# Seven quarter products for eight in three of eight blocks of a quantized FFN's second product, the residual added by GpSimd, and some waits rearranged

## What is computed

```python
fused = concat([x, mean(x, axis=1), cond, cond], -1)         # 4 x 1024 x 1536
r = relu(fused @ cond_W + cond_b)                            # 512 wide
h = relu(quant_linear(r, w1, b1))                            # FFN1: 512 -> 2048
y = quant_linear(h, w2, b2)                                  # FFN2: 2048 -> 512
out = x + y
def quant_linear(x, w, b):
    s_in = max(x) / 255;  xq = clip(round(x / s_in), 0, 255) * s_in
    s_w  = rowmax(|w|) / 127;  wq = clip(round(w / s_w), -128, 127) * s_w
    return xq @ wq.T + round(b / (s_in * s_w)) * (s_in * s_w)
```

## Time and profile before

| what | us |
|---|---|
| median of 3 executions (326.12 to 329.09) | 326.31 |
| the profiled execution, its own device time | 326.76 |
| its span in the profile | 325.0 |
| PE busy (share of the span) | 315.9 (97%) |
| DVE busy | 256.5 (79%) |
| ACT busy | 205.3 (63%) |
| POOL busy | 95.2 (29%) |

### The profile page before, as it was taken

The page is one execution under the profiler, slowest core; times in us unless marked ns, Lnnn a source line. Parts: engine busy times, 40 slices in busy tenths (PEclk is TensorE's granted clock), DMA queues, the critical chain, the costliest instruction groups (busy, mean ns, idle before and its releaser), DMA issues.

```text
span 325.0 us, 4331 instructions
## 1 busy us (share of the span) xinstructions
PE 315.9 (97%) x1491; PEld 180.3 (55%) x1491; DVE 256.5 (79%) x541; ACT 205.3 (63%) x364; POOL 95.2 (29%) x80
## 2 busy tenths in 40 slices
PE   6999999999998999999999999899999999999995
PEld 6888888888685444444444444344444444444444
DVE  1698988997888999999999999844569665665665
ACT  2445695578376993466666663199996959568300
POOL 1076524644223999970370002600000000000000
PEclk9999999999999999999999999999999999999999
DMA  7999999999963397995990150379969799567042
GB/s 224 207 248 245 231 194 242 258 244 321 310 126 68 66 275 35 356 417 243 416 419 7 70 192 0 131 304 422 408 233 415 287 357 382 175 221 289 0 161 99
DMA packets 51622, 75.54 MB, mean 232 GB/s; under 512 B 20344, under 2 KB 34960, under 8 KB 46864
## 3 DMA queue, kind: packets, MB, share of 16 engines
q1 hardware_dynamic: 51408, 74.99, 76.7%
q10 hardware_dynamic: 192, 0.28, 0.4%
HBM read 45.89 MB, written 25.17 MB: 219 GB/s over the span
## 4 chain that ended last, share of the span: by engine, by line
PE 79%; DVE 11%; DMA 4%; issue 2%; ACT 1%; SPq 1%; DVEq 0%
PE bank L734 34%; PE bank L632 20%; PE bank L507 17%; PE bank L604 6%; DMA pool_q<-in_L_ffn_w_dram 2%; DVE wmax L927 2%; DVE hidden L1049 2%; DMA x_in<-in_x_dram 1%; SPq L304 1%; DVE hidden L910 1%; PE bank L502 1%; DVE hidden L915 1%; DVE pool_r L1024 1%; DVE w_sum L992 1%; ACT pool_r L790 1%
## 5 line engine op out<-in xcount | busy, mean ns | idle before, releaser
L734 PE MATMUL bank<-w_t,pool_q 128*128 128x512 f16 x256 | 55.9, 379 | 0.2 <-DVE pool_q L1144 0.2
L734 PE MATMUL bank<-w_t 128*128 128x512 f16 (+1 forms) x272 | 55.9, 366 | 0.0
L1159 DVE TENSOR_TENSOR bank<-bank,ends_b 128x512 f32<-128x512 f32 (+1 forms) x33 | 22.5, 681 | 38.8 <-PE bank L734 38.7
L1049 DVE TENSOR_SCALAR_CACHE_REDUCE hidden<-bank,qb,hmax 128x512 f32<-128x512 f32 x62 | 47.6, 809 | 4.4 <-PE bank L632 3.8
L424 POOL TENSOR_TENSOR x_lo<-hidden,x_hi 128x512 fp32r<-128x512 f32 x28 | 35.4, 1300 | 45.5 <-ACT x_hi L771 45.5
L507 PE MATMUL bank<-x_lo,cw_hi 128*128 128x512 f32 x128 | 48.4, 389 | 0.0
L507 PE MATMUL bank<-x_hi,cw_lo 128*128 128x512 f32 x128 | 48.4, 389 | 0.0
L507 PE MATMUL bank<-x_hi,cw_hi 128*128 128x512 f32 x128 | 48.2, 392 | 0.1
L1069 DVE CUSTOM_DVE_ANT_0 hidden<-hidden,bank,hmax 128x512 f32<-128x512 f32 x66 | 45.9, 743 | 0.1
L875 ACT ACTIVATE w_t<-hidden,s_quant 128x512 uint8<-128x512 f32 x64 | 39.6, 710 | 7.8 <-PE bank L734 7.8
L875 ACT ACTIVATE pool_q<-hidden,s_quant 128x512 uint8<-128x512 f32 x63 | 39.0, 711 | 7.1 <-PE bank L734 7.0
(11 more groups left out here) (131 smaller groups left out, 403.4 us busy)
## 6 DMA issues: line engine op xcount, KB each, us to landing
hidden_spill<-hidden SPq DMA_DIRECT2D x16, 1024.0 KB, 10.9
hidden<-hidden_spill SPq DMA_DIRECT2D x16, 1024.0 KB, 7.8
x_in<-in_x_dram SPq DMA_DIRECT2D x32, 256.0 KB, 7.0
pool_r<-in_x_dram SPq DMA_DIRECT2D x8, 1024.0 KB, 5.5
pool_q<-in_L_ffn_w_dram SPq DMA_DIRECT2D x7, 1024.0 KB, 10.3
out_dram<-pool_r SPq DMA_DIRECT2D x7, 1024.0 KB, 8.6
pool_r<-in_L_cond_W_dram SPq DMA_DIRECT2D x2, 1024.0 KB, 10.2
x_in<-in_L_ffn_w_dram SPq DMA_DIRECT2D x1, 1024.0 KB, 5.3
```

The lines of the kernel that those rows point to most:

```text
L734: return pe.matmul(y_bank[:, cols], hid_q[n % 2][:, ft, j * P:(j + 1) * P], w2_t[:, ft, cols], start=(ft == 0), stop=(ft == FT - 1))
L1049: dve.tensor_scalar(hidden[:, at:at + TB], y_bank[:, :], qb1[:, ft:ft + 1], hmax[:, ft:ft + 1], ALU.add, ALU.max, accum_out=hmax[:, ft:ft ...
L1159: step(dve.tensor_tensor(y, y, b2_b[:, cols], ALU.add))
```

## The change

Blocks 2, 4 and 6 of FFN2 (`FOLDED`) are computed by `folded`. The hidden block is cut into quarters a11, a12, a21, a22 (token half, feature half), w2 into B11, B12, B21, B22 (feature half, output half). Seven products of quarters, some of them of sums of quarters, replace eight. Each product is 8 matmuls of 256 columns for a group of 128 tokens, so a folded block is 2 x 7 x 8 = 112 matmuls of 256 columns. Their order for each of the two token groups is: 1 (a11 B11), 5 (HS0 W2S0), 6 (HS1 W2S1, added to 1's bank), 3 (HS3 B22, added to 5's bank), 7 (HS2 W2S2, on 1's bank), 2 (a12 B21), 4 (a22 W2S3, on 1's bank). Where a bank is added to further, DVE first takes out a copy of what it holds (`fold_taken`).

DVE makes the four sums of w2's quarters once (`W2S`, 2048 f16 elements a partition each), and for each folded block the four sums of hidden quarters in two halves (`sum_hidden`, four instructions of 1024 f16 elements for each half). All of these have both inputs in SBUF; the second and third of a half wait for the end of the one before. They lie in the SBUF slot of hidden block 0, so only three slots are left for reloads (`SLOT`), and the reloads wait for whole blocks.

`finish` keeps its bias instruction and writes the scaled bank to SBUF rows (`out_rows`, in `steps`) instead of the bank; POOL adds these rows to the residual (28 additions of 512 f32 elements, `summed`). The last block is finished by DVE as before. `finish_folded` has seven instructions of 256 elements and two of 512 (both inputs in SBUF) for each of the two token groups. In a pair of blocks n (plain, odd) and n + 1 (folded) DVE's order is written out: finish 0 and 1 of n, first half of the sums, finish 2, second half of the sums, `finish_folded` with finish 3 of n inside.

Half of hidden block 1 is quantized by DVE (8 instructions) in place of ACT. PE computes block 1 token group by token group. ACT's order of tiles for a folded block is such that the first 8 serve the first half of the sums.

Waits ahead of FFN2: DVE's multiplication of w1's row sums goes from ahead of `bias1` (L992) to the end of the `qb1` computation. POOL fills slices 2 to 5 first, as soon as `bias_done` allows, then slice 1; its last two fills, and the `sum_w` after them, wait for `qb_ready`. The maximum over `h` is multiplied and reduced after the last tile, with the instruction L1136 gone.

The diff, cut to its core:

```diff
+        FOLDED = (2, 4, 6)
+        PLAIN = [n for n in range(NB) if n not in FOLDED]
+        SLOT = (0, 1, 2, 3, 1, 2, 3, 1)
+        sums_h = hidden[:, 0:HB].bitcast(F16).rearrange("p (w s f c) -> p w s f c", w=2, s=4, f=FG)
+        W2S = [sums_h[:, 0, i] for i in range(4)]
+        HS = [sums_h[:, 1, i] for i in range(4)]
+        B11, B12, B21, B22 = (w2_t[:, f * FG:(f + 1) * FG, c * HALF:(c + 1) * HALF] for f in range(2) for c in range(2))
+        def hid_quarters(n):
+            return [hid_q[n % 2][:, f * FG:(f + 1) * FG, t * HALF:(t + 1) * HALF] for t in range(2) for f in range(2)]
+        out_rows = steps[:, :, :, :].rearrange("p a b t -> p (a b t)").bitcast(F32).rearrange("p (j d) -> p j d", d=D)
+        ROWS = [(0, 2, 1, 3) if n in FOLDED else (0, 1, 2, 3) for n in range(NB)]
+        FIRST = slice(0, HALF)
+        LAST = slice(HALF, TB)
+        F1, F5, F2 = (bank[0], bank[3]), bank[1], bank[2]
+        HG = FG // 2
+        folded_tiles = [h * HG + f + g * FG for h in range(2) for g in range(2) for f in range(HG)]
+        ACT_TILES = [list(range(1, FT)), list(range(FG, FT))]
+        ACT_TILES += [folded_tiles if n in FOLDED else list(range(FT)) for n in range(2, NB)]
         def tiles_to(n):
-            return n * FT - 1 if n else -1
+            return sum(len(tiles) for tiles in ACT_TILES[:n])
...
             def reload(n):
+                if n == SLOTS:
+                    sp.wait_ge(first_hid_ready, 2 + FG)
+                    sp.wait_ge(hid_ready, tiles_to(2))
+                else:
+                    sp.wait_ge(hid_ready, tiles_to({5: 3, 6: 4, 7: 5}[n]))
                 for q in range(FQ):
-                    sp.wait_ge(hid_ready, tiles_to(n) + 4 * (q + 1))
-                    sp.dma_start(hidden[:, n * HB + q * 4 * TB:n * HB + (q + 1) * 4 * TB],
-                                 spill[n, :, q * 4 * TB:(q + 1) * 4 * TB]).then_inc(reloaded[n % 2], 16)
+                    sp.dma_start(hidden[:, SLOT[n] * HB + q * 4 * TB:SLOT[n] * HB + (q + 1) * 4 * TB],
+                                 spill[n - SLOTS, :, q * 4 * TB:(q + 1) * 4 * TB]).then_inc(reloaded[n % 2], 16)
 
             def store(n):
                 slot = n % SLOTS
-                sp.wait_ge(y_taken, TJ * (n + 1))
+                sp.wait_ge(summed, TJ * (n + 1))
...
-            pool.wait_ge(w_turned[1], 16 * (NB // 2 - 1))
-            fill(pool_r, 1, act_filled)
             pool.wait_ge(bias_done, 1)
             for i in range(2, 6):
                 fill(pool_r, i, act_filled)
+            pool.wait_ge(w_turned[1], 16 * (NB // 2 - 1))
+            fill(pool_r, 1, act_filled)
+            pool.wait_ge(qb_ready, 1)
...
+            for n in range(NB - 1):
+                pool.wait_ge(xres_landed[n % 2], 16 * (n // 2 + 1))
+                for r, j in enumerate(ROWS[n]):
+                    xs = x_res[:, n % SLOTS * WC + j * D:n % SLOTS * WC + (j + 1) * D]
+                    pool.wait_ge(scaled, TJ * n + r + 1)
+                    pool.tensor_tensor(xs, xs, out_rows[:, j, :], ALU.add).then_inc(summed, 1)
...
+            def folded(n):
+                a11, a12, a21, a22 = hid_quarters(n)
+                before = 2 * 7 * FOLDED.index(n)
+                sums = 8 * FOLDED.index(n)
+                def part2(i, a, b, to, start=False, stop=False):
+                    for f in range(FG):
+                        mm = pe.matmul(to[:, 0:HALF], a[:, f, i * P:(i + 1) * P], b[:, f, :],
+                                       start=(start and f == 0), stop=(f == FG - 1), skip_group_check=not start)
+                    mm.then_inc(fold_done, 1)
+                for i in range(2):
+                    done = before + 7 * i
+                    if i == 0:
+                        if before == 0:
+                            pe.wait_ge(scaled, TJ)
+                        else:
+                            pe.wait_ge(fold_taken, before)
+                        pe.wait_ge(hid_ready, tiles_to(n + 1))
+                    part2(i, a11, B11, F1[i], start=True)
+                    if i == 0:
+                        pe.wait_ge(w2s_ready, 4)
+                        pe.wait_ge(hs_ready, sums + 5)
+                    else:
+                        pe.wait_ge(fold_taken, done - 3)
+                    part2(i, HS[0], W2S[0], F5, start=True)
+                    pe.wait_ge(fold_taken, done + 1)
+                    if i == 0:
+                        pe.wait_ge(hs_ready, sums + 6)
+                    part2(i, HS[1], W2S[1], F1[i])
+                    pe.wait_ge(fold_taken, done + 2)
+                    if i == 0:
+                        pe.wait_ge(hs_ready, sums + 7)
+                    part2(i, HS[3], B22, F5)
+                    pe.wait_ge(fold_taken, done + 3)
+                    if i == 0:
+                        pe.wait_ge(hs_ready, sums + 8)
+                    part2(i, HS[2], W2S[2], F1[i])
+                    if i == 1:
+                        pe.wait_ge(fold_taken, done - 1)
+                    part2(i, a12, B21, F2, start=True)
+                    pe.wait_ge(fold_taken, done + 5)
+                    part2(i, a22, W2S[3], F1[i])
...
+                elif n - 2 in FOLDED:
+                    act.wait_ge(fold_done, 2 * 7 * (FOLDED.index(n - 2) + 1))
+                for ft in ACT_TILES[n]:
...
-            dve.wait_ge(w_h_ready, KD)
-            step(dve.tensor_scalar(w1_sum[:, :], w1_sum[:, :], -OFFSET, None, ALU.mult))
...
-            step(dve.tensor_tensor(qb1[:, :], qb1[:, :], w1_sum[:, :], ALU.add))
-            dve.sem_inc(qb_ready, 1)
+            dve.wait_ge(w_h_ready, KD)
+            step(dve.tensor_scalar(w1_sum[:, :], w1_sum[:, :], -OFFSET, None, ALU.mult))
+            dve.tensor_tensor(qb1[:, :], qb1[:, :], w1_sum[:, :], ALU.add).then_inc(qb_ready, 1)
+            dve.wait_ge(qb_ready, 1)
...
-                if i == 7:
-                    dve.wait_ge(h_taken, BANKS + 2 * FT + 7)
-                    dve.wait_ge(c12_taken, GROUPS)
-                    dve.wait_ge(c21_taken, GROUPS)
-                    step(dve.tensor_tensor(htop[:, :], hmax[:, :], s1[:, :], ALU.mult))
-                    step(dve.tensor_reduce(col[:, :], htop[:, :], AX.X, ALU.max))
...
-            dve.tensor_scalar(col[:, :], hmax[:, FT - 1:FT], s1[:, FT - 1:FT], col[:, 0:1], ALU.mult, ALU.max
-                              ).then_inc(top_ready, 1)
+            dve.wait_ge(c12_taken, GROUPS)
+            dve.wait_ge(c21_taken, GROUPS)
+            step(dve.tensor_tensor(htop[:, :], hmax[:, :], s1[:, :], ALU.mult))
+            dve.tensor_reduce(col[:, :], htop[:, :], AX.X, ALU.max).then_inc(top_ready, 1)
...
+            dve.wait_ge(hid_filled, 8)
+            for ft in range(FG):
+                dve.tensor_scalar(hid_low[1][:, ft, :], hidden[:, HB + ft * TB:HB + (ft + 1) * TB],
+                                  s1[:, ft:ft + 1], s_h_inv[:, 0:1], ALU.mult, ALU.mult).then_inc(first_hid_ready, 1)
+            dve.wait_ge(first_hid_ready, 2)
+            dve.wait_ge(hid_ready, tiles_to(1))
+            dve.tensor_tensor(W2S[0], B12, B11, ALU.subtract).then_inc(w2s_ready, 1)
+            dve.wait_ge(w2s_ready, 1)
+            dve.tensor_tensor(W2S[1], B22, W2S[0], ALU.add).then_inc(w2s_ready, 1)
+            dve.tensor_tensor(W2S[2], B22, B12, ALU.add).then_inc(w2s_ready, 1)
+            dve.wait_ge(w2s_ready, 2)
+            dve.tensor_tensor(W2S[3], B21, W2S[1], ALU.subtract).then_inc(w2s_ready, 1)
+            def row_free(n, j):
+                if n > 0:
+                    dve.wait_ge(summed, TJ * (n - 1) + ROWS[n - 1].index(j) + 1)
+            def finish(n, j):
+                y = bank[TJ * (n % 2) + j][:, :]
+                dve.wait_ge(y_done, TJ * PLAIN.index(n) + j + 1)
+                step(dve.tensor_tensor(y, y, b2_b, ALU.add))
+                row_free(n, j)
+                dve.tensor_tensor(out_rows[:, j, :], y, s2_b, ALU.mult).then_inc(scaled, 1)
+            def sum_hidden(n, h):
+                at = slice(h * HG, (h + 1) * HG)
+                a11, a12, a21, a22 = (a[:, at, :] for a in hid_quarters(n))
+                t1, t2, t3, t4 = (a[:, at, :] for a in HS)
+                count = 8 * FOLDED.index(n) + 4 * h
+                dve.wait_ge(hid_ready, tiles_to(n) + FG * (h + 1))
+                dve.wait_ge(fold_done, 2 * 7 * FOLDED.index(n))
+                dve.tensor_tensor(t1, a21, a22, ALU.subtract).then_inc(hs_ready, 1)
+                dve.wait_ge(hs_ready, count + 1)
+                dve.tensor_tensor(t2, a11, t1, ALU.subtract).then_inc(hs_ready, 1)
+                dve.wait_ge(hs_ready, count + 2)
+                dve.tensor_tensor(t4, a12, t2, ALU.subtract).then_inc(hs_ready, 1)
+                dve.tensor_tensor(t3, a21, a11, ALU.subtract).then_inc(hs_ready, 1)
+            def finish_folded(n, between):
+                before = 2 * 7 * FOLDED.index(n)
+                for i in range(2):
+                    top, low = out_rows[:, i, :], out_rows[:, 2 + i, :]
```

(34 more changed lines are left out.)

82 lines of the change are left out of this document (43 added, 39 removed).

## The result

The changed kernel takes 329.60 us (median of 8 runs, 329.38 to 330.55). The kernel before, run beside it, takes 326.65 us (8 runs). The ratio is 1.0085 with a 95% interval of 1.0058 to 1.0112: slower by 0.9%, less than the 1% that the prediction took as the least change to be told. Forecast were 327.7 us and no change. A ratio leaves out an execution that lies more than 1.5% above the fastest of its kernel (one of run 4, one of run 8) and is worked out from all the others, so it can differ a little from the quotient of the medians. The profiled execution of after took 329.62 us with a span of 327.8; before's had 325.0. The 2.8 us between the spans are what has to be found.

The account below looks back on a forecast made before the run. FFN2 was taken as bound by PE without a gap. FFN2 +3.3 (-4.8 matmuls, +8.1 idle) and -1.9 ahead of it give +1.4 us on 326.31: 327.7 us, no change, range 319.5 to 330.0.

Parts of the forecast that it names:

- A: Main theory: DVE instructions with two SBUF inputs wait while POOL adds; 327.7 us, own range 326.5 to 329.7, chance 0.45.
- FFN2 bound by PE without a gap: In FFN2, PE runs 110.73 us in one piece, so every microsecond of PE there counts in full.
- Matmuls, -4.8: A folded block takes PE 12.2 us in place of 13.8; three of them give -4.8 us.
- The collision: POOL's additions hold DVE's sums and scalings; PE idles 2.7 us a folded block, 8.1 us in three.
- FFN2 +3.3: FFN2's sum: -4.8 us from matmuls and +8.1 us from idle time give +3.3 us.
- Ahead of FFN2, -1.9: Gains before FFN2: -1.0 moved scaling, -0.6 POOL kept out until `qb_ready`, -0.3 at FFN1's end; -1.9 us.
- the moved scaling (-1.0): With L992 moved away, L1017 no longer stands behind POOL's memsets and starts on PE: -1.0 us.
- POOL's wait (-0.6): POOL kept out until `qb_ready` removes DVE's stalls in the bias computation and PE's idle time ahead of L604: -0.6 us.
- Edits at nothing: DVE's half of block 1, w2's sums, ACT's quantizing, later reloads, POOL's additions and the tail cost no time.
- rival C: In a chain of sums DVE isn't held by POOL; folded blocks idle some 0.2 us: 320.2 us, chance 0.25.
- B: Rival: POOL runs beside DVE's first sum and only DVE waits; a folded block idles 2.0 us: 325.6 us, chance 0.18.
- D: Rival: DVE's sums run at one element a cycle, each half 2.1 us more: 344 us, chance 0.07.

Follow-up runs that it names:

- run 4: Run 3 with the plain blocks' rows also taken as 0, 2, 1, 3, nothing left out: 324.94 us, ratio 0.9943 to the kernel before.
- run 8: The kernel before with only the scaling of w1's row sums moved: 328.37 us, ratio 1.0057 to the kernel before.
- run 5: Run 4 with each reload issued right behind a store, ahead of its landing and the load of x: 322.11 us, ratio 0.9871 to the kernel before.
- run 1: The changed kernel with POOL's 28 residual additions replaced by memsets of the same rows: 326.13 us, ratio 0.9964 to the kernel before.
- run 2: The changed kernel with POOL's additions of a plain block's rows 1 and 2 held until the following half of the sums is through: 328.81 us, ratio 1.0076.
- run 3: Run 2 with a folded block's first row of each token group also held until the second is scaled: 326.23 us, ratio 1.0001 to the kernel before.
- run 9: Run 1 (POOL only writes) with the early reloads of run 5: 321.31 us, ratio 0.9836 to the kernel before.
- run 7: The kernel before with only the three edits ahead of FFN2 (moved scaling, POOL's fills and wait, last peak): 325.52 us, ratio 0.9983.

## Why the prediction was right, step by step

The class (no change) and the mechanism were right. The size was 1.5 us short: +1.4 forecast, +2.95 measured between the medians. The two terms that were off, FFN2 and the head, erred the same way. The 329.60 us lie just inside A's own range (to 329.7) and at the limit that was given for slower by over 1% (329.57, from 326.31); against the kernel before run beside it, 326.65, they are 0.9% more. So the class was right by little. By its steps:

- **FFN2 bound by PE without a gap.** Right. Run by run the time follows PE's waits in FFN2.
- **Matmuls, -4.8.** Right in kind, short in size: a folded block is 12.46 us without stalls (run 5), not 12.2, so three give -4.1. In run 5's first folded block most groups start 0.87 to 0.88 us apart, 8 x 0.109; one lies 0.93 behind its forerunner, and the two pairs that read `hidden` take 1.79 and 1.87 us for 1.75. What this 0.2 us in all is was not tried.
- **The collision.** Right in place, order and length: the second sum 1.64 us (forecast over 1.5), half a set 3.61 (3.6), the second scaling held 1.60 - 0.69 = 0.91 (0.8), idle 1.90 ahead of product 6 (1.8) and 1.01 in the second token group (0.8). A folded block loses 15.25 - 12.46 = 2.8 us; forecast 2.7. Runs 1 to 5 and 9 show that the additions cause it.
- **FFN2 +3.3** became +4.3. Of the 1.0 us, 0.7 is the matmuls' term and 0.3 the stalls'.
- **Ahead of FFN2, -1.9** became -1.4. L1118 began 0.6 us earlier and not 1.0: PE's last relation product was itself at 100.74 for 100.47, behind a weight chunk that landed later, and L1118 began 0.54 us behind it, where the forecast had 0.43. The idle time ahead of L604 went; by the starts of L619 and L604 and of their counterparts in after (L666, L651) it was 0.8 us (5.96 for 5.18), not 0.6. The 0.3 at FFN1's end came (0.2) and was given back: FFN2's first matmul stood 0.37 us for L1242 (0.16 before). The prediction priced the moved scaling (-1.0) and POOL's wait (-0.6) as two gains; run 8, in which the first alone is slower than the kernel before, shows no gain of the first without the second. The -1.4 is that of one pair of traces: the nine profiled kernels with this head begin FFN2 at 208.98 to 210.13 us, later where SP's transfers run later, and run 7's median lies only 0.75 us below the kernel before.
- **Edits at nothing.** The sums of w2 ended at 223.0 us (forecast 224.4), DVE's half of block 1 at 217.9. Of the reloads it named blocks 4's and 6's as the tightest; it was block 7's. In the changed kernel this cost nothing. With run 4's reload taking 294.6 - 279.0 = 15.6 us, where the prediction had about 12, an estimate for after is 277.9 + 15.6 = 293.5, 1.7 us ahead of need. So the nearly gap-free 320.2 of rival C could not have been reached by this kernel; by run 1, C was worth some 326.
- **The rivals.** B (POOL runs beside DVE's sum) falls with POOL's record of 1.65 us and its late end, C with the 1.64 of L1290, D with 0.69 for every sum of 1024 elements that meets no addition. Two figures there don't fit their own terms, without weight in the sum: C's half 1 would end at about 15.0 (8.45 + 2.6 + 1.34 + 2.6), not 14.5, and the folded finish is 7.5 to 8.9 us, of which only the low end was taken.

On C the prediction had weighed the Trainium skill (SBUF — State Buffer, A bandwidth-pool intuition that's wrong), which has the blocked side start about 115 ns after DVE's end; by that, DVE's next sum, 0.04 us behind, would win. The trace disagrees: DVE's first sum ended at 232.19, the second's record starts at 232.23, and it stood until POOL was through, six times in FFN2 (1.64 to 1.65 us each). The other rule cited, also of the Trainium skill (VectorE: DVE Perf Modes, The perf-mode tier table), two f16 elements a cycle, is borne out by 0.69 us for 1024 elements and 1.22 for 2048: 0.53 us for 1024 more, about half the one-element slope of 1.0 us per 1000.

## What to carry to other kernels

Before work is handed to GpSimd, look at what DVE does when it is released: an addition begun just ahead of a chain of DVE instructions with two SBUF inputs added three quarters of its length to that chain here (0.95 of 1.27 us), and the release of both by one event made it happen every time. Holding the addition back helps only if what it reads is not needed next. When a stall is taken out, ask of every transfer and every buffer what the stall had covered: here it was worth 3 to 5 us (runs 4 to 5 and 1 to 9), as much as the matmuls saved in two or three blocks. And an instruction moved off one path stands on another; count what it meets there.
